# Moving router and norms to GpSimd, spreading the softmax's inverse by TensorE, and reordering ScalarE's and GpSimd's slots

## The chip, the cores and the metric

One core of a Trainium2 chip runs the whole kernel. The metric is the device time in microseconds; lower is better. An execution here takes about 6.4 milliseconds.

## The reference

The input x is 8 images of 56 x 56 positions with 64 channels, fp32. Four blocks follow each other, each added to its input:

1. Attention over regions. The normed input is projected to q, k and v. Each image has 7 x 7 regions of 64 positions. For each region the 4 best regions are chosen by the product of mean q and mean k. With 8 heads of 8 channels, each of the 64 queries scores the 256 keys of these four regions, keeps the **32 largest scores** (`jax.lax.top_k`), and takes the softmax over these 32 alone to mix the values. A 3 x 3 depthwise convolution of v is added, then an output projection.
2. A mixture of 8 experts over tokens: logits by a router, softmax, the two largest probabilities, scaled so that their sum is 1; out = t + sum over experts of weight * (gelu(t @ w1 + b1) @ w2 + b2), with t the layer norm of the tokens.
3. A 3 x 3 convolution with weights of +1 and -1 on the normed input.
4. Another mixture of 8 experts, with a hidden size of 128 and a router with a bias, where the two largest probabilities are used as they are.

## The kernel before, in words

The image rows are cut into 56 strips of 8 rows (448 positions, 4 tiles of 112), seven strips an image. A strip holds 7 regions, so there are 392 regions. Time is laid out in **slots**: one region is selected a slot. Two strips (14 slots) are a turn, and a hardware loop runs over turns.

Five kinds of work share the slots:
- stage a (strip): norm, q/k/v projection, stores to DRAM;
- stage t (strip): choice of the four regions;
- stage b (region): gather k, v and q (sp_gather), scores on TensorE (pe_scores), copy to b_s (act_scores), selection on VectorE (dve_select: four rounds of MAX8 and MATCH_REPLACE8 on four blocks of 256 keys, where a selected score becomes GONE), softmax sum (act_sum: negated maximum, four exponentials of the 32 kept values with an accumulated sum) and exponentials of all scores (act_exp), then on GpSimd the inverse of the sum (pool_inverse, L493, a power of -1), the mask (pool_mask, L502: is the score GONE, times the inverse, four instructions since the inverse is a column for each block of heads), the product (pool_prob, L510), then the turn of the probabilities by TensorE in two halves (pe_turn L524, copies act_turn L532) and the values (pe_values L545, copy act_values L552);
- stage c0 (strip, a few slots later): depthwise convolution and output projection (step 0 of pe_c, L611 to L616), turned back to tokens (TURN), added to x (L816), norm, router (GATE, step 3, step 4), experts in groups (UP + g, DOWN + g), sum, second norm, split into bf16 parts (step 8, LOW);
- stage c1 (strip): binary convolution (L619 to L623), the same norm, router and experts, store.

What is done in which slot is a table, PLACES: for each engine a number per step. The whole part, taken modulo 7, is the slot; the fraction is the place in it. In `("c0", 4): 85.7` for VectorE, 85 is slot 1 modulo 7. Experts have their own rows: c0's groups stand in slots 86 and 87 (2 and 3 modulo 7), c1's in slots 110, 111 and 112 (5, 6 and 0). Each engine works through its list in order, and waits on semaphores. The order inside one slot r:
- VectorE: dve_select(r), then its steps. It waits for the scores of r and for the product of r-2 (b_prob), since b_r and b_v8 have two buffers.
- ScalarE: act_sum(r), act_exp(r), steps below 0.2, first copy of the turned probabilities of r-1, act_scores(r + 2), second copy, steps to 0.6, act_values(r - 1), the rest of the steps.
- TensorE: steps below 0.2, pe_turn(r - 1, 0), pe_scores(r + 2), pe_turn(r - 1, 1), steps to 0.6, pe_values(r - 1), the rest.
- GpSimd: pool_inverse(r), pool_mask(r), steps from 0.2 to 0.5, pool_prob(r), the rest.

On VectorE stages c0 and c1 have step 1 (tok = x + projection, mean and variance), step 2 (normalise, L247 and L251), step 3 (largest logit and subtraction), step 4 (router: L834 to L861, some 18 operations of 32 or 4 columns), step 7 (sum and second statistics). ScalarE's step 3 is the router's exponential (L728). An exponential after a GELU, and a GELU after an exponential, needs an ACT_TABLE_LOAD; plain copies do not.

## Time and profile before

| | |
|---|---|
| runs shown | 6418.39, 6423.66, 6434.80 us; median 6423.66 |
| profiled execution | 6440.11 us, its span 6438.2 us |
| busy: PE, DVE, ACT, POOL | 4737.3, 5596.4, 4054.4, 4425.8 us |
| share of the span | 74%, 87%, 63%, 69% |
| granted TensorE clock | 0.73 of full over the span |
| chain that ended last | PE 29%, ACT 18%, issue 16%, DVE 15%, POOL 12% |
| HBM | 34 GB/s over the span |

The busy times are of one profiled execution; an engine's instructions may overlap each other, and such overlap is counted once in the busy share, but twice where the time of a group of instructions is summed. The chain is the one followed back from the last instruction; "issue" in it is time in which the profile shows no wait.

### The profile page before, as it was taken

How to read it: one execution, taken by the hardware profiler on the slowest of the kernel's cores; microseconds unless marked ns; L12 is line 12 of the kernel's file. 1: busy time of each engine (PE TensorE's matmuls, PEld its weight loads, DVE VectorE, ACT ScalarE, POOL GpSimd, SP SyncE). 2: the span in 40 equal slices, each digit the busy share in tenths (PEclk: the TensorE clock that was granted, in tenths of full speed). 3: DMA queues.
4: the chain of work that ended last, by engine and by line, in shares of the span. 5: the costliest groups of instructions: out<-in, count | busy, mean ns of one | idle time of the engine just before them, and what ended most of it. 6: DMA issues, size and time to landing. Idle time of an engine off the chain costs nothing.

```text
span 6438.2 us, 135940 instructions
## 1 busy us (share of the span) xinstructions
PE 4737.3 (74%) x26938; PEld 2880.6 (45%) x26938; DVE 5596.4 (87%) x24453; ACT 4054.4 (63%) x10222; POOL 4425.8 (69%) x3986
## 2 busy tenths in 40 slices
PE   3566777777777777777777777777777777777776
PEld 1333444444444444444444444444444444444444
DVE  1999999988989998999989898989999899999941
ACT  2455666666666666666666666666666666666643
POOL 1667776767677776767677677767776777777742
PEclk9666767777777777777777777777777777777777
DMA  4111111111111111111111111111111111111100
GB/s 75 39 31 42 34 40 34 40 32 42 30 41 34 39 35 34 40 32 43 32 42 30 40 36 36 38 33 40 32 43 31 43 31 32 30 30 34 33 11 10
DMA packets 585501, 229.09 MB, mean 36 GB/s; under 512 B 481152, under 2 KB 580224, under 8 KB 584576
## 3 DMA queue, kind: packets, MB, share of 16 engines
q1 hardware_dynamic: 584576, 219.25, 15.4%
q8 instruction: 276, 4.52, 0.3%
q14 instruction: 649, 5.32, 0.3%
HBM read 150.14 MB, written 68.80 MB: 34 GB/s over the span
## 4 chain that ended last, share of the span: by engine, by line
PE 29%; ACT 18%; issue 16%; DVE 15%; POOL 12%; ACTq 0%; DVEq 0%; POOLq 0%; DMA 0%; SPq 0%
DVE b_v L452 7%; POOL b_r L502 5%; PE y_ps L685 4%; DVE b_r L463 4%; PE h_ps L611 4%; POOL c_h L762 4%; ACT b_x L478 3%; PE a_ps L666 3%; PE pT_ps L524 3%; PE o_ps L545 2%; ACT b_e L485 2%; ACT L737 2%; PE h_ps L666 2%; POOL b_rec L493 2%; ACT L478 2%
## 5 line engine op out<-in xcount | busy, mean ns | idle before, releaser
L463 DVE MATCH_REPLACE8 b_r<-b_v,b_r 128x256 f32<-128x256 f32 x4704 | 1879.1, 416 | 0.0
L502 POOL TENSOR_SCALAR b_r<-b_r,b_rec 128x256 f32<-128x256 f32 x1568 | 1777.1, 1147 | 119.6 <-POOL b_rec L493 119.6
L452 DVE MAX8 b_v<-b_r 128x8 f32<-128x256 f32 x4704 | 1649.2, 418 | 0.0
L524 PE MATMUL pT_ps<-k_ident,b_e 128*128 128x128 f32 x3136 | 669.9, 352 | 776.3 <-ACT b_pT L532 688.3
L493 POOL TENSOR_TENSOR b_rec<-b_den,k_mone 128x4 f32<-128x4 f32 x392 | 400.5, 1022 | 1153.5 <-ACT b_x L478 1150.2
L762 POOL TENSOR_TENSOR c_h<-c_h,c_cb 128x448 f32<-128x448 f32 x672 | 760.9, 1133 | 503.9 <-ACT c_cb L739 503.0
L524 PEld LDWEIGHTS pT_ps<-k_ident,b_e 128*128 128x128 f32 x3136 | 472.6, 180 | 1161.2 <-issue 1136.2
L510 POOL TENSOR_TENSOR b_e<-b_e,b_r 128x1024 f32<-128x1024 f32 x392 | 923.5, 2356 | 18.0 <-POOL b_r L502 14.4
L685 PE MATMUL y_ps<-k_w,c_h 128*112 128x64 f32 x5376 | 776.1, 298 | 181.1 <-POOL c_h L762 177.9
L685 PEld LDWEIGHTS y_ps<-k_w,c_h 128*112 128x112 f32 x5376 | 706.5, 210 | 404.1 <-issue 403.0
L452 DVE MAX8 b_v<-b_s 128x8 f32<-128x256 f32 x1568 | 551.1, 415 | 318.0 <-POOL b_e L510 201.2
L532 ACT ACTIVATE b_pT<-pT_ps 128x512 f32<-128x512 f32 x784 | 469.9, 599 | 432.3 <-PE pT_ps L524 432.0
L485 ACT ACTIVATE b_e<-b_s,b_nm 128x256 f32<-128x256 f32 x1568 | 662.1, 493 | 0.0
L463 DVE MATCH_REPLACE8 b_r<-b_v,b_s 128x256 f32<-128x256 f32 x1568 | 624.7, 413 | 0.0
L666 PE MATMUL h_ps<-c_xT,k_w 128*128 128x448 f32 x672 | 525.4, 879 | 74.0 <-issue 67.5
L425 PE MATMUL s_ps<-b_k,b_q 32*128 32x256 f32 x3136 | 559.5, 484 | 24.2 <-DMA b_q<-q_d 24.2
L435 ACT ACTIVATE b_s<-s_ps 128x512 f32<-128x512 f32 x784 | 427.0, 603 | 117.5 <-PE s_ps L425 117.3
L478 ACT ACTIVATE b_x<-b_v,b_nm 128x32 f32<-128x32 f32 x1568 | 484.2, 310 | 9.5
L666 PE MATMUL a_ps<-c_xT,k_w 128*128 128x448 f32 x672 | 451.5, 765 | 0.0
L425 PEld LDWEIGHTS s_ps<-b_k,b_q 32*128 32x128 f32 x3136 | 336.3, 233 | 155.7 <-issue 119.6
L463 DVE MATCH_VALUE_LOAD b_r<-b_v,b_r 128x8 f32 x4704 | 405.3, 86 | 0.0
L737 ACT ACTIVATE c_h<-h_ps,k_b 128x448 f32<-128x448 f32 x336 | 212.8, 633 | 271.2 <-PE h_ps L666 268.5
(146 smaller groups left out, 7904.9 us busy)
## 6 DMA issues: line engine op xcount, KB each, us to landing
q_d<-a_qe SPq DMA_DIRECT2D x56, 448.0 KB, 4.2
b_k<-k_d SPq DMA_DIRECT2D x1568, 16.0 KB, 2.0
b_v<-v_d SPq DMA_DIRECT2D x1568, 16.0 KB, 2.0
b_q<-q_d SPq DMA_DIRECT2D x392, 64.0 KB, 2.1
c_win<-vpad_d SPq DMA_DIRECT2D x56, 145.0 KB, 2.8
c_hm<-cpad_d SPq DMA_DIRECT2D x56, 145.0 KB, 2.3
vpad_d<-a_vT SPq DMA_DIRECT2D x56, 116.0 KB, 3.7
c_win<-vpad_d SPq DMA_DIRECT2D x56, 116.0 KB, 2.7
```

The costliest lines, as they stand in the source:

```text
L425: last = pe.matmul(s_ps[g][:, t * NKEY:(t + 1) * NKEY], b_q[r % RING][part, 2 * t:2 * t + 2, :].rearrange("c h t -> c (h t)"), b_k[r % RIN ...
L452: top = dve.max(out=b_v8[p][:, t, 8 * rnd:8 * rnd + 8], in_=src[:, t, :])
L463: last = dve.match_replace(out=b_r[p][:, t, :], in_to_replace=b_v8[p][:, t, 8 * rnd:8 * rnd + 8], in_values=src[:, t, :], imm_value=GONE)
L478: last = act.activation(b_x8[:, t, :], b_v8[p][:, t, :], ACT.Exp, bias=b_nm[p][:, t:t + 1], accum_out=b_den[p][:, t:t + 1])
L485: last = act.activation(b_e[p][:, t, :], b_s[p][:, t, :], ACT.Exp, bias=b_nm[p][:, t:t + 1])
L493: pool.tensor_tensor(out=b_rec[p][:, :], in0=b_den[p][:, :], in1=k["mone"][:, 0:HP], op=ALU.pow).then_inc(b_inv, 1)
L502: last = pool.tensor_scalar(out=b_r[p][:, t, :], in0=b_r[p][:, t, :], scalar1=GONE, scalar2=b_rec[p][:, t:t + 1], op0=ALU.is_le, op1=ALU.mult)
L510: pool.tensor_tensor(out=b_e[p][:, :, :], in0=b_e[p][:, :, :], in1=b_r[p][:, :, :], op=ALU.mult).then_inc(b_prob, 1)
L524: last = pe.transpose(pT_ps[:, col:col + 128], b_e[p][:, t, c * 128:(c + 1) * 128], k["ident"][:, :])
L666: pe.matmul(bank[:, 0:STRIP], w1[layer][:, g, :], D["xT"][:, :], start=True, stop=True).then_inc(S["h"], 1)
L685: last = pe.matmul(y_ps[0:TILE, t * C:(t + 1) * C], D["h"][g % 2][:, t * TILE:(t + 1) * TILE], w2[layer][:, g, :], start=False, stop=(g == ...
L762: pool.tensor_tensor(out=D["h"][g % 2][:, :], in0=D["h"][g % 2][:, :], in1=D["cb"][g % 2][:, :], op=ALU.mult).then_inc(S["hc"], 1)
```

## The change

- Stage b: the inverse of the sum moves from GpSimd to VectorE (dve_inverse, a reciprocal), placed inside the selection of the **next** region, after its first four MAX8. The mask on GpSimd is one instruction over 1024 elements without the inverse. The product is therefore not normalised; instead TensorE spreads the inverses of a region over the rows of o_ps beside the values (four products with the identity), act_values copies 256 columns, and GpSimd multiplies a whole strip once (c0 step NORM).
- ScalarE and GpSimd: the steps and the turned probabilities of region r-1 come first, act_sum(r), act_exp(r) and act_scores(r + 2), or pool_mask(r) and pool_prob(r), last.
- Stages c0 and c1: addition (ADD), norm and residual are done on GpSimd. Router: ScalarE copies the logits into a padded tile, VectorE only takes the eight largest and replaces the two largest (MAX8 and MATCH_REPLACE8 over 14 columns); GpSimd subtracts, and after one exponential over both copies takes the difference, which leaves the two chosen; then sum, inverse and split into bf16 parts, nine small operations in a chain.
- PLACES: norm transposes and gates one slot earlier on TensorE and ScalarE, the layer-0 convolution from before the turned probabilities of slot 1 to behind its values, the router's exponential from 0.7 to 0.3 of a slot (of slot 6 to slot 5, and of slot 3 to slot 2), and others as in the diff.

```diff
-        b_rec = [sb(f"b_rec{i}", [128, HP]) for i in range(2)]
+        b_rec = [sb(f"b_rec{i}", [128, HP]) for i in range(RING)]
-        b_at = [sb(f"b_at{i}", [128, 2, RH, W]) for i in range(2)]
+        b_at = [sb(f"b_at{i}", [128, 4, RH, W]) for i in range(2)]
...
+        def dve_inverse(dve, tau, r):
+            reg = tau * SLOTS + r
+            dve.wait_ge(b_sum, reg + 1)
+            alone(dve)
+            dve.reciprocal(b_rec[r % RING][:, :], b_den[r % 2][:, :]).then_inc(b_inv, 1)
...
+                if rnd == 0 and older is not None:
+                    dve_inverse(dve, tau, older)
...
-            for t in range(HP):
-                last = pool.tensor_scalar(out=b_r[p][:, t, :], in0=b_r[p][:, t, :], scalar1=GONE, scalar2=b_rec[p][:, t:t + 1],
-                                          op0=ALU.is_le, op1=ALU.mult)
-            last.then_inc(b_msk, 1)
+            pool.tensor_scalar(out=b_r[p][:, :, :], in0=b_r[p][:, :, :], scalar1=GONE, scalar2=None,
+                               op0=ALU.is_le).then_inc(b_msk, 1)
...
             pe.wait_ge(b_att, reg + 1)
             alone(pe)
+            pe.wait_ge(b_inv, reg + 1)
+            alone(pe)
+            for t in range(HP):
+                pe.matmul(o_ps[32 * t:32 * t + VH, 128:256], b_rec[r % RING][:, t:t + 1].broadcast_to([128, VH]), k["ident"][:, :],
+                          start=True, stop=True)
...
-                           o_ps[:, 0:128].rearrange("c (j h q) -> c j h q", j=2, h=RH), ACT.Copy).then_inc(b_att, 1)
+                           o_ps[:, 0:256].rearrange("c (j h q) -> c j h q", j=4, h=RH), ACT.Copy).then_inc(b_att, 1)
...
-                    pe.wait_ge(b_att, NWIN * (s + 1) + 1)
+                    pe.wait_ge(b_nrm, s + 1)
...
-                act.activation(D["p"][:, :, :], D["l"][:, :, :], ACT.Exp).then_inc(S["ex"], 1)
+                act.activation(D["p"][:, :, :, :], D["l"][:, :, :, :], ACT.Exp).then_inc(S["ex"], 1)
...
+            if step == NORM:
+                pool.wait_ge(b_att, NWIN * (s + 1) + 1)
+                pool.tensor_tensor(out=b_at[i][:, 0:2], in0=b_at[i][:, 0:2], in1=b_at[i][:, 2:4], op=ALU.mult).then_inc(b_nrm, 1)
+            if step == ADD:
+                pool.wait_ge(S["x_in"][i], LOADS[layer] * (tau + 1))
+                pool.wait_ge(S["pr"], s + 1)
...
+                pool.tensor_tensor(out=D["tok"][i][:, :, :], in0=D["x"][i][:, :, :], in1=D["pr"][:, :, :], op=ALU.add).then_inc(S["free"], 1)
...
+                normalise(pool, D["tok"][i], D["mv"], D["rs"], D["xn"], S["sub"], s + 1, S["norm"])
...
+            if step == 3:
+                pool.wait_ge(S["top"], s + 1)
+                alone(pool)
+                pool.tensor_tensor(out=D["l"][:, :, :, :], in0=D["lr"][:, :, :, 0:NE],
+                                   in1=D["pv"][:, :, 6:7].unsqueeze(1).broadcast_to([TILE, 2, NT, NE]), op=ALU.subtract).then_inc(S["ls"], 1)
+            if step == 4:
...
+                pool.wait_ge(S["ex"], s + 1)
+                alone(pool)
+                pool.tensor_tensor(out=cw[:, :, :], in0=p[:, 0], in1=p[:, 1], op=ALU.subtract).then_inc(mix, 1)
...
             if step == 3:
                 dve.wait_ge(S["lc"], s + 1)
                 alone(dve)
...
+                lr, pv = D["lr"], D["pv"]
                 for t in range(NT):
-                    ins = dve.max(out=D["pv"][:, t, :], in_=p[:, t, :])
+                    ins = dve.max(out=pv[:, t, :], in_=lr[:, 0, t, :])
                 link(ins)
                 for t in range(NT):
...
+                    ins = dve.match_replace(out=lr[:, 1, t, :], in_to_replace=pv[:, t, :], in_values=lr[:, 0, t, :], imm_value=GONE)
+                ins.then_inc(S["top"], 1)
...
-                ("c1", 0): 101.66, ("c1", 9): 115.66},
-            dve={("a", 1): 4.9, ("a", 5): 10.9, ("t", 2): 61.8,
-                 ("c0", 1): 80.7, ("c0", 2): 81.7, ("c0", 3): 83.7, ("c0", 4): 85.7, ("c0", 7): 89.7,
-                 ("c1", 1): 104.66, ("c1", 2): 106.66, ("c1", 3): 108.66, ("c1", 4): 109.66, ("c1", 7): 114.66},
-            pool={("a", 1): 4.9, ("c0", 1): 80.7, ("c0", 2): 81.7, ("c0", 7): 89.7, ("c0", 8): 91.7, ("c1", 1): 104.66},
+                ("c1", 0): 101.66, ("c1", 9): 114.66},
+            dve={("a", 1): 4.9, ("a", 5): 10.9, ("t", 2): 60.8,
+                 ("c0", 1): 79.7, ("c0", 3): 81.7, ("c0", 7): 88.7,
+                 ("c1", 1): 103.7, ("c1", 3): 106.7, ("c1", 7): 113.7},
+            pool={("a", 1): 5.2, ("c0", NORM): 78.2, ("c0", ADD): 79.25, ("c0", 1): 80.2, ("c0", 3): 82.25, ("c0", 4): 82.35,
+                  ("c0", 7): 89.2, ("c0", 8): 90.2,
+                  ("c1", ADD): 103.25, ("c1", 1): 104.2, ("c1", 3): 107.25, ("c1", 4): 107.35},
             pe={("a", 3): 7.9, ("a", 4): 8.9, ("t", 1): 59.8,
-                ("c0", 0): 78.1, ("c0", TURN): 78.5, ("c0", TURNED): 78.68, ("c0", 2): 81.66, ("c0", GATE): 82.05,
...
+                ("c0", 0): 78.62, ("c0", TURN): 78.7, ("c0", TURNED): 78.8, ("c0", 2): 80.75, ("c0", GATE): 81.05,
+                ("c0", GATED): 81.31, ("c0", 4): 85.85, ("c0", 8): 92.3, ("c0", LOW): 92.55, ("c0", LOWED): 92.69,
+                ("c1", 0): 102.1, ("c1", TURN): 102.5, ("c1", TURNED): 102.68, ("c1", 2): 105.695, ("c1", GATE): 106.05,
...
-                 ("c0", 0): 78.3, ("c0", TURN): 78.52, ("c0", 2): 81.68, ("c0", GATE): 82.12, ("c0", 3): 83.7,
...
+                 ("c0", 0): 78.64, ("c0", TURN): 78.72, ("c0", 2): 80.77, ("c0", GATE): 81.12, ("c0", 3): 82.3,
+                 ("c0", 4): 85.87, ("c0", 8): 92.35, ("c0", LOW): 92.57,
+                 ("c1", 0): 102.3, ("c1", TURN): 102.52, ("c1", 2): 105.7, ("c1", GATE): 106.12, ("c1", 3): 107.3,
...
                     for r in range(SLOTS):
                         before = on and (r >= 1 or not first)
-                        if on:
-                            act_sum(act, b, r)
-                            act_exp(act, b, r)
                         steps(act, "act", n, lo, r, fs, 0, 0.2)
                         if before:
                             act_turn(act, b, r - 1, 0)
-                        if on and (r + 2 < SLOTS or not last):
-                            act_scores(act, b, r + 2)
-                        if before:
                             act_turn(act, b, r - 1, 1)
...
                         steps(act, "act", n, lo, r, fs, 0.6, 1)
+                        if on:
+                            act_sum(act, b, r)
+                            act_exp(act, b, r)
+                            if r + 2 < SLOTS or not last:
+                                act_scores(act, b, r + 2)
...
                     for r in range(SLOTS):
+                        steps(pool, "pool", n, lo, r, fs, 0, 1)
                         if on:
-                            pool_inverse(pool, b, r)
                             pool_mask(pool, b, r)
-                        steps(pool, "pool", n, lo, r, fs, 0.2, 0.3)
-                        steps(pool, "pool", n, lo, r, fs, 0.3, 0.5)
-                        if on:
                             pool_prob(pool, b, r)
-                        steps(pool, "pool", n, lo, r, fs, 0.5, 1)
```

## Rows read from the trace of the kernel before

**Rows 1.** Stretch 3000 to 4000 us: length, busy by engine (count), clock, DMA, GB/s.

```profile
3000.00:4000.00 1000.00, 757.00 (x4368) 462.21 (x4367) 901.51 (x3924) 658.71 (x1652) 713.77 (x642) 0.72 0.16 36
```

**Rows 2.** Power L493, once a region: whole span, then two stretches (length, busy, count).

```profile
L493 POOL TENSOR_TENSOR b_rec<-b_den,k_mone x392: 1006/1016/1274, 170.9 to 6164.2; 128x4 f32<-128x4 f32 x196
...
3000.00:4000.00 1000.00, 64.24 (x63) 0.72 0.16 36
5200.00:5400.00 200.00, 14.28 (x14) 0.77 0.15 35
```

**Rows 3.** VectorE in order of time, one selection and the steps behind it.

```profile
3063.07 1.41 DVE L452 MAX8 b_v<-b_s 128x8 f32<-128x256 f32 x4 [0.53 <-issue]
...
3074.60 2.23 DVE L247 TENSOR_TENSOR c_xn<-c_tok,c_mv 112x256 f32<-112x256 f32 x1
...
3082.46 1.41 DVE L452 MAX8 b_v<-b_s 128x8 f32<-128x256 f32 x4
...
3091.10 1.41 DVE L452 MAX8 b_v<-b_r 128x8 f32<-128x256 f32 x4
```

**Rows 4.** VectorE's waits, 3000 to 4000 us: total us, times, longest.

```profile
DVE b_v L452 <- POOL b_e L510: 46.9, 9, 5.7
```

**Rows 5.** ScalarE in order of time, sums and first or second copies.

```profile
3063.07 0.19 ACT L475 ACTIVATE b_nm<-b_v 128x4 f32<-128x4 f32 x1
...
3070.47 0.60 ACT L532 ACTIVATE b_pT<-pT_ps 128x512 f32<-128x512 f32 x1
...
3080.07 0.21 ACT L475 ACTIVATE b_nm<-b_v 128x4 f32<-128x4 f32 x1
...
3089.67 0.60 ACT L532 ACTIVATE b_pT<-pT_ps 128x512 f32<-128x512 f32 x1 [5.14 <-PE pT_ps L524]
...
3101.00 0.20 ACT L475 ACTIVATE b_nm<-b_v 128x4 f32<-128x4 f32 x1
```

**Rows 6.** ScalarE's waits, 3000 to 4000 us, then (last row) 5200 to 5900 us.

```profile
ACT b_pT L532 <- PE pT_ps L524: 69.0, 49, 5.2
...
ACT b_nm L475 <- DVE b_v L452: 46.3, 9, 5.7
ACT c_h L737 <- PE h_ps L666: 42.7, 22, 3.5
...
ACT b_nm L475 <- DVE b_v L452: 45.7, 18, 4.8
```

**Rows 7.** ScalarE by line and shape, 3000 to 4000 us: busy, mean ns, idle before.

```profile
L485 ACT ACTIVATE b_e<-b_s,b_nm 128x256 f32<-128x256 f32 x252 | 106.4, 493 | 0.0
L478 ACT ACTIVATE b_x<-b_v,b_nm 128x32 f32<-128x32 f32 x252 | 77.8, 310 | 1.5
...
L737 ACT ACT_TABLE_LOAD x45 | 57.7, 1283 | 0.8
```

**Rows 8.** TensorE in order of time: turns and scores at either clock.

```profile
3020.88 0.66 PE L524 MATMUL pT_ps<-k_ident,b_e 128*128 128x128 f32 x4
3021.47 1.13 PE L425 MATMUL s_ps<-b_k,b_q 32*128 32x256 f32 x8
...
3031.92 1.06 PE L524 MATMUL pT_ps<-k_ident,b_e 128*128 128x128 f32 x4
3032.91 2.08 PE L425 MATMUL s_ps<-b_k,b_q 32*128 32x256 f32 x8
```

**Rows 9.** GpSimd by line and shape, 3000 to 4000 us.

```profile
L502 POOL TENSOR_SCALAR b_r<-b_r,b_rec 128x256 f32<-128x256 f32 x252 | 285.8, 1148 | 19.2 <-POOL b_rec L493 19.2
L510 POOL TENSOR_TENSOR b_e<-b_e,b_r 128x1024 f32<-128x1024 f32 x64 | 150.7, 2355 | 2.9 <-POOL b_r L502 2.9
...
L775 POOL CAST c_x<-c_xm 112x256 bf16<-112x256 f32 x9 | 3.6, 396 | 1.8 <-POOL c_xm L251 1.8
```

**Rows 10.** GpSimd in order of time: first and last operation of step 8.

```profile
3076.51 0.80 POOL L247 TENSOR_TENSOR c_xm<-c_x,c_mv 112x256 f32<-112x256 f32 x1
...
3080.14 0.72 POOL L782 TENSOR_TENSOR c_x<-c_xd,c_x 112x256 bf16<-112x256 f32 x1
```

132 lines of the change are left out of this document (55 added, 77 removed).

## The prediction

> **What bounds the kernel now.** I read the stretch view first [rows 1], because the page's shares are means: between 3000 and 4000 us every stage is on, VectorE is busy 90% of the time, GpSimd 71%, ScalarE 66%, TensorE 76% at a granted clock of 0.72, a mix of its two levels, 1.2 and 2.4 GHz. VectorE looks like the bound. The count of regions gives the pace [rows 2]: 63 in 1000 us, 15.87 us a region slot, 111.1 us a strip of seven. In the last part, where stage a has ended, 14 slots take 200 us, 100 us a strip. Of 392 slots the full load holds from about slot 112 to 394 (40.3 strips) and the lighter one to 462 (9.7 strips).
>
> A selection runs from 3063.07 to 3074.60 [rows 3]: 11.5 us, 81 us a strip. So VectorE would have 30 us a strip to spare, and the change takes most of that off it. The question is what holds it back at present. Its waits name GpSimd's product of probabilities [rows 4]: 46.9 us in nine strips, one wait of 5.2 us a strip. Behind that stands ScalarE. The selection that began at 3082.46 had its last maxima at about 3092.5 [rows 3], and ScalarE began that region's softmax only at 3101.00 [rows 5]: 8.5 us late. ScalarE waits for VectorE 46.3 us in nine strips [rows 6], once a strip; the rest of its idle time is spent on TensorE (turned probabilities 69.0, hidden layer 42.7). So **ScalarE's own chain is 111.1 - 5.1 = 106.0 us a strip**, only 5 us under the pace, though it is busy for 73. VectorE hides its lateness only because a region's result is wanted a whole slot later (two buffers). In the last part the same sum is 100 - 6.5 = 93.5 us [rows 2, 6].
>
> **VectorE.** Removed: both norms, the additions of tokens and the router's arithmetic. One such block lies between 3074.60 and 3082.46, 7.9 us, 2.2 of it a subtraction that stood against GpSimd's product [rows 3]. With the other layer I take 13.5 us a strip. Added: a reciprocal a region (0.2 each, the nearest being the router's small ones) and four small replacements a layer, 2.6 us together. Its pace would be 7 x 11.7 + 9 = 91 us a strip. But the edit also moves a wait: the reciprocal of region r-1 stands after the first four maxima of region r (1.4 us), and waits for ScalarE's sum r-1. VectorE may now be ahead of ScalarE by some 3 us, not by a slot. And ScalarE's sum r wants VectorE's last maxima, 8.6 us after that reciprocal. Behind the waiting reciprocal the whole rest of the selection is queued.
>
> **ScalarE's chain, the term that decides.** It stays in order: older work of slot r, then sum r, exponentials r, scores r+2. What each edit adds to its 106.0 us a strip:
> 1. *Table loads, +5.1.* The router's exponential now stands at 0.3 of slots 5 and 2, between GELUs at 0.15 and 0.35; before, it stood last and shared the load of the region's softmax. That makes two more loads for each of two layers, 4 x 1.283 [rows 7]. Nothing hides them: ScalarE is the chain.
> 2. *Turning region r at once, +7.5 in the five slots with GELUs.* Before, from the end of a sum (3063.07 + 1.5 without a load) to the end of the second copy (3071.07) went 6.5 us [rows 5], since the product had been ready for long. Now: exponentials 1.69 [rows 7], product 2.36 [rows 9], 0.2 of signals, a turn of 0.6, scores 1.1, a turn 0.6, a copy 0.6, makes 7.2 at the full clock; with 1.0, 2.1 and 1.0 for the TensorE pieces at the low one 9.0 [rows 8]. So +0.7 to +2.5 a slot; I take 1.5, the clock now being mixed. Bounds 3.5 to 12.5. The GELU at 0.15 with its load fills the wait for the product, else it would be more.
> 3. *The two slots without GELU at the head, +2.4*, by the same sum without the filler, less what they waited before; bounds 0 and 5.
> 4. *The layer-0 convolution behind the values, +1.5.* Before, ScalarE did a sum and exponentials (3080.07 on) under it and then waited 5.14 us [rows 5]. Now it stands idle for all of it, 5.2 to 8.0 us; bounds 0 and 2.9.
> 5. *Two copies at 0.35 and 0.57 of slot 1 that wait for each other through TensorE, +0.9*; bounds 0 and 1.5.
> 6. *Wider values copy (256 columns for 128), +0.7.* The four spreading products on TensorE (0.3 to 0.5 us a region) start before the second copy is there; I cost them at nothing, their cover being that copy.
> 7. *GpSimd in slot 6, +4.0.* At 0.2 stand the splitting of layer 0 (3076.51 to 3080.86, 4.35 us [rows 10]) and the norm of layer 1 (one power of 1.02, two passes of some 0.7, small ones and signals, 2.9), ahead of the first hidden product. That comes 8 us after the region's product, TensorE's first down-projection of the slot some 4 us later than ScalarE would let it, and the third GELU stands behind it. Bounds 2 and 5.
> 8. *A credit, -2.4.* The hidden products no longer stand behind mask and product of the same region; of the 42.7 us in which ScalarE waited for h_ps (4.7 a strip [rows 6]) I take half. Bounds 0 and -4.7.
>
> The sum is +19.7, bounds +6.6 and +32.7 with all at one end.
>
> **GpSimd.** The four masks of 1148 ns and the power of 1.02 us a region become one mask of 1024 elements. No row shows this form. Below: four casts of 256 elements, 1.6 us; above: the four masks, 4.6 [rows 9]. I take 1.6, since what has no operand from a column in memory is nearest to the cast. It lies under ScalarE's late softmax at either value in four slots, and is late by up to 1.8 us in slots 3, 6 and 0. The router (nine small operations, some 3.9 us with their waits, twice), the additions, norms and the product NORM come to 13 us; the engine is busy 79.3 - 39.2 + 11.2 + 13 = 64 us a strip. Its cover is ScalarE's chain of 125. The router's wait for the exponential holds up the second hidden product of slots 5 and 2; what is late there is the end of TensorE's slot, 16 us in, and the next GELU has 2 us in hand.
>
> **SyncE.** The DMAs are the same; one store stands a slot earlier, beside a DMA share of 0.16 [rows 1]. Nothing.
>
> **The numbers.** ScalarE's chain becomes 106.0 + 19.7 = 125.7 us a strip, above VectorE's 91: 14.6 more than 111.1. In the last part 93.5 + 19.7 = 113.2, 13.2 more. 40.3 x 14.6 + 9.7 x 13.2 = 588 + 128 = 716 us. The profiled execution took 6440.1 us (span 6438.2); the median of the runs shown is 0.26% below it. 7156 x 0.9974 = 7138, and with a few us back in the tail, where VectorE's router chain was in the path, **7130 us**. With each term at its lower end the strip takes 112.6 us: about 6500 us. At the upper end 138.7 us: 7800 us.
>
> Of table loads the Trainium skill (ScalarE: Activation LUTs, What ACT_TABLE_LOAD costs) says that a switch costs a drain besides, 2.66 us in all. By that the four would cost 10.6 us a strip, and the time would be 7400 us. The rows speak against it here: 252 activations behind such loads had 1.5 us of idle time before them in all [rows 7].
>
> **Rivals.** *VectorE sets the pace (17%), the faster side.* If ScalarE keeps within 3 us of VectorE in the five light slots (2 to 6), only slots 0 and 1 stay long (18.8 and 21.5 us at the full clock) and the others take 5 x 11.7 + 8: 107 us a strip, and 100 in the last part. That is 40.3 x -4.1 = -165: 6260 us. It decides at 13 us for ScalarE's light slots, where I find 15 to 20. For it speaks the 30 us that VectorE gains, against it row upon row of ScalarE waiting for TensorE, with just one wait a strip for VectorE.
> *The waits change places (6%).* TensorE stays at 2.4 GHz since its gaps become shorter, the credit is whole, and 6440 us stays. The granted 0.72 speaks against it: the wait for the product is a new gap of 2 to 3 us in each slot.
> *GpSimd's single mask costs as much as four (10%).* Then it is late in three slots, 1.8 us each: 5.4 x 50 = 270, so 7400 us. If the mask does not become shorter the change does not do what it says.
> The forecast has 67%. About 0.3%, 20 us, is what a measurement of this kernel can tell from no change.
>
> Faster by more: 17% and 1% of the places case, 0.18. Within 0.3%: 0.05. Slower: 0.77. The forecast's own range is 6650 to 7500. To leave out no more than two in ten the lower end goes down to 6350, which takes in the waits case and the lower bounds, but not the whole of the faster rival: 6350 to 7500.
>
> **What would show it.** Right: in the changed profile ScalarE has 14 table loads a strip (before, 45 of nine strips stand at the GELUs, and as many bring the exponential back: 10), its first softmax operation hardly waits for VectorE's maxima, VectorE idles at its new reciprocal for ScalarE's sum (some 30 us a strip, the longest in slot 2, behind the convolution), VectorE's share falls to 75%, and 63 slots take over 1100 us. The mask reads 1.2 to 1.8 us. Wrong: VectorE stays above 95% busy and ScalarE waits for its maxima in most slots; then the chain of step 2 was shorter than the rows made it, or lay beside something. If the time is right but ScalarE waits for GpSimd's products, step 7 was too small and step 2 too large.

## The result, and the profile after

The changed kernel takes **7863.5 us** in the median of four runs (7858.9 to 7873.7), the kernel before, run beside it, 6426.6 us (6418.4 to 6434.8): ratio 1.2238, interval 1.2217 to 1.2259, 1437 us more. The direction was forecast. The time was not: 7130 us stood in the forecast, and 7500 as its upper end.

The page of the changed kernel: its span, the busy times of part 1, TensorE's clock from part 2 and five groups of part 5 (busy, mean ns of one, idle before, what ended it):

```profile
span 7860.9 us, 141661 instructions
...
PE 5294.8 (67%) x30074; PEld 3185.7 (41%) x30074; DVE 5008.0 (64%) x22719; ACT 4439.8 (56%) x10426; POOL 4023.5 (51%) x4042
...
PEclk9565666666666666666666666666666666677666
...
L522 PE MATMUL pT_ps<-k_ident,b_e 128*128 128x128 f32 x3136 | 846.2, 424 | 1371.3 <-POOL b_e L508 1354.4
L508 POOL TENSOR_TENSOR b_e<-b_e,b_r 128x1024 f32<-128x1024 f32 x392 | 922.3, 2353 | 1631.9 <-ACT b_e L494 1617.3
...
L443 DVE RECIPROCAL b_rec<-b_den 128x4 f32<-128x4 f32 x392 | 68.6, 175 | 2356.4 <-ACT b_x L487 2356.3
L501 POOL TENSOR_SCALAR b_r<-b_r 128x1024 f32<-128x1024 f32 x392 | 1087.0, 2773 | 741.2 <-DVE b_r L472 736.8
...
L530 ACT ACTIVATE b_pT<-pT_ps 128x512 f32<-128x512 f32 x784 | 468.7, 598 | 1457.0 <-PE pT_ps L522 1457.0
```

No engine is the bound any more: the fullest, TensorE, is busy 67% of the span at a low clock, VectorE fell from 87% to 64%. The four large idle sums are links of one ring. ScalarE's copy waits for TensorE's turn, the turn for GpSimd's product, the product for ScalarE's exponentials, and VectorE's reciprocal for ScalarE's sum. All of a region's softmax is now done in one line, at each slot anew.

The same stretch of 1000 us as in [rows 1], and the masks in it, which count regions as the powers of [rows 2] did:

```profile
3000.00:4000.00 1000.00, 693.70 (x3961) 417.89 (x3960) 652.35 (x2952) 589.50 (x1370) 532.08 (x536) 0.67 0.13 29
...
3000.00:4000.00 1000.00, 144.21 (x52) 0.67 0.13 29
```

There were 63 regions, now there are 52: 19.2 us a slot for 15.9. Over all 392 regions, from the first mask at 174.6 us to the last at 7564.4, a slot takes 18.90 us; before, from 170.9 to 6164.2, it took 15.33. Those 3.57 us times 391 are 1396 of the 1437.

Waits of the changed kernel, 3000 to 4000 us (total, times, longest):

```profile
DVE b_rec L443 <- ACT b_x L487: 327.7, 44, 14.4
...
POOL b_e L508 <- ACT b_e L494: 219.4, 36, 15.6
ACT b_pT L530 <- PE pT_ps L522: 182.0, 97, 2.8
PE pT_ps L522 <- POOL b_e L508: 153.8, 51, 5.9
```

ScalarE's wait for turned probabilities was 69.0 us, 49 times, in [rows 6]. It now comes at nearly every copy. The 46.3 us in which it waited for VectorE's maxima are no longer in the list. The engines in order of time (start, length; in brackets the idle time before):

```profile
3004.00 0.20 ACT L484 ACTIVATE b_nm<-b_v 128x4 f32<-128x4 f32 x1
...
3006.74 1.69 ACT L494 ACTIVATE b_e<-b_s,b_nm 128x256 f32<-128x256 f32 x4
...
3009.12 2.35 POOL L508 TENSOR_TENSOR b_e<-b_e,b_r 128x1024 f32<-128x1024 f32 x1 [0.16 <-POOL b_r L501]
...
3011.86 1.08 PE L522 MATMUL pT_ps<-k_ident,b_e 128*128 128x128 f32 x4 [2.46 <-POOL b_e L508]
...
3012.99 0.60 ACT L530 ACTIVATE b_pT<-pT_ps 128x512 f32<-128x512 f32 x1 [1.06 <-PE pT_ps L522]
3016.04 0.60 ACT L530 ACTIVATE b_pT<-pT_ps 128x512 f32<-128x512 f32 x1 [2.46 <-PE pT_ps L522]
...
3069.10 0.63 ACT L716 ACTIVATE c_yT<-h_ps,out_bias 64x448 f32<-64x448 f32 x1 [6.77 <-PE h_ps L620]
...
3077.50 0.18 DVE L443 RECIPROCAL b_rec<-b_den 128x4 f32<-128x4 f32 x1 [14.06 <-ACT b_x L487]
```

From the end of the sum (3006.84) to the end of the second copy (3016.64) go 9.8 us; six such stretches in a row read 9.2 to 10.1, where I had 7.2 at the full clock and 9.0 at the low one. The mean over the 1000 us is 9.4; before, it was 6.8. In five of the six the two copies start 3.05 or 3.06 us apart, as here, and the first turn takes 1.08 us: TensorE turns both halves at the low level. At the convolution ScalarE stands 6.77 us, and VectorE stands 14.06 at the reciprocal.

**Two halves of a slot.** For what follows I cut ScalarE's slots between 3000 and 3992 us into two: A from the start of the negated maximum to the end of the second turned copy, B from there to the next negated maximum. Means in us, worked out from each run's timeline (the changed kernel's A and B sum to 19.5 where the count of masks gives 19.2, so 0.3 us is what such a mean is good for):

| kernel | us | A | B |
|---|---|---|---|
| before (62 slots) | 6432 | 8.97 | 6.93 |
| changed (50) | 7864 | 11.91 | 7.61 |
| before with new orders (45) | 8785 | 15.81 | 6.00 |
| changed, old orders (52) | 7423 | 8.74 | 9.76 |
| changed, old places (53) | 7435 | 12.27 | 5.89 |
| changed, idle transposes (52) | 7595 | 11.03 | 7.73 |
| combination (63) | 6259 | 8.84 | 6.56 |

"Orders" are those of ScalarE and GpSimd. "Old places" are those of router, norms and first convolution; step 7, step 8 and the store keep the places of the change.

### The profile page after: what moved, and what is told of

It is laid out like the page before. It is cut to its first block and busy times, and to the rows that moved or that the text cites. A ratio compares the mean times of both kernels' runs of the same rounds, so it can differ in the third digit from the quotient of the medians.

```text
span 7860.9 us, 141661 instructions
## 1 busy us (share of the span) xinstructions
PE 5294.8 (67%) x30074; PEld 3185.7 (41%) x30074; DVE 5008.0 (64%) x22719; ACT 4439.8 (56%) x10426; POOL 4023.5 (51%) x4042
## 5 line engine op out<-in xcount | busy, mean ns | idle before, releaser
L522 PE MATMUL pT_ps<-k_ident,b_e 128*128 128x128 f32 x3136 | 846.2, 424 | 1371.3 <-POOL b_e L508 1354.4
L443 DVE RECIPROCAL b_rec<-b_den 128x4 f32<-128x4 f32 x392 | 68.6, 175 | 2356.4 <-ACT b_x L487 2356.3
L501 POOL TENSOR_SCALAR b_r<-b_r 128x1024 f32<-128x1024 f32 x392 | 1087.0, 2773 | 741.2 <-DVE b_r L472 736.8
L522 PEld LDWEIGHTS pT_ps<-k_ident,b_e 128*128 128x128 f32 x3136 | 549.0, 213 | 1919.9 <-issue 1919.9
L689 PE MATMUL y_ps<-k_w,c_h 128*112 128x64 f32 x5376 | 812.3, 308 | 412.1 <-POOL c_h L813 404.7
L689 PEld LDWEIGHTS y_ps<-k_w,c_h 128*112 128x112 f32 x5376 | 760.2, 221 | 623.9 <-issue 617.6
L425 PE MATMUL s_ps<-b_k,b_q 32*128 32x256 f32 x3136 | 803.2, 661 | 24.2 <-DMA b_q<-q_d 24.2
L670 PE MATMUL a_ps<-c_xT,k_w 128*128 128x448 f32 x672 | 563.3, 941 | 0.0
L425 PEld LDWEIGHTS s_ps<-b_k,b_q 32*128 32x128 f32 x3136 | 455.8, 314 | 216.9 <-issue 150.1
L741 ACT ACTIVATE c_h<-a_ps,k_b 128x448 f32<-128x448 f32 x336 | 213.2, 635 | 371.6 <-PE a_ps L670 369.7
```

Of the source, the lines that this page charges most:

```text
L425: last = pe.matmul(s_ps[g][:, t * NKEY:(t + 1) * NKEY], b_q[r % RING][part, 2 * t:2 * t + 2, :].rearrange("c h t -> c (h t)"), b_k[r % RIN ...
L501: pool.tensor_scalar(out=b_r[p][:, :, :], in0=b_r[p][:, :, :], scalar1=GONE, scalar2=None, op0=ALU.is_le).then_inc(b_msk, 1)
L522: last = pe.transpose(pT_ps[:, col:col + 128], b_e[p][:, t, c * 128:(c + 1) * 128], k["ident"][:, :])
L670: pe.matmul(bank[:, 0:STRIP], w1[layer][:, g, :], D["xT"][:, :], start=True, stop=True).then_inc(S["h"], 1)
L689: last = pe.matmul(y_ps[0:TILE, t * C:(t + 1) * C], D["h"][g % 2][:, t * TILE:(t + 1) * TILE], w2[layer][:, g, :], start=False, stop=(g == ...
L741: act.activation(D["h"][g % 2][:, :], (h_ps, a_ps)[g % 2][:, 0:STRIP], ACT.Gelu, bias=b1[layer][:, g:g + 1]).then_inc(S["ge"], 1)
```

## The experiments

Except for e15, each kernel was run once beside the kernel before (6427.5 to 6432.4 us). Where PLACES is edited, the diffs here show only the entries that differ.

**e1, ScalarE's old order in the changed kernel.**

```diff
+                        if on:
+                            act_sum(act, b, r)
+                            act_exp(act, b, r)
                         steps(act, "act", n, lo, r, fs, 0, 0.2)
                         if before:
                             act_turn(act, b, r - 1, 0)
+                        if on and (r + 2 < SLOTS or not last):
+                            act_scores(act, b, r + 2)
+                        if before:
                             act_turn(act, b, r - 1, 1)
...
-                        if on:
-                            act_sum(act, b, r)
-                            act_exp(act, b, r)
-                            if r + 2 < SLOTS or not last:
-                                act_scores(act, b, r + 2)
```

> The changed kernel with ScalarE's old order alone: sum and exponentials of region r first, then the slot's steps, with the scores' copy between the two copies of the turned probabilities of r-1. GpSimd keeps the new order. Theory A (ScalarE's chain is the pace, and the new order puts softmax, product and turn of one region behind each other in it): the wait for the product and the gap between the two copies leave the chain, some 2.5 to 3.5 us a slot, so about 6700 to 7000 us, and ScalarE's waits for turned probabilities fall from 25 us a strip below 12. Rival B (VectorE's slack is gone, since the reciprocal stands inside the selection): the reciprocal still waits there, 7700 us or more.

Measured: 7334.4 us, 529 less, though not down to the 6700 to 7000 of theory A. The wait for turned copies fell from 182.0 to 34.2 us, the clock rose from 0.673 to 0.705. But 906 us stayed, in new waits: VectorE's router maxima for ScalarE's logits (84.6 us), GpSimd's addition of tokens for ScalarE's copy (92.9). So the order costs, and is not all.

**e3, the reciprocal behind the third round of maxima** (`rnd == 0` becomes `rnd == 2`).

> The changed kernel with the reciprocal of region r-1 behind the maxima of the third round of region r instead of the first, so that VectorE can be 5.8 us further ahead before it waits. Theory A: VectorE's wait shrinks, but ScalarE is the chain and the time stays within 1% of 7860 us. Rival B: VectorE's wait is the cost, and the time falls by 30 us a strip, to 6400 to 6800 us.

Measured: 7852.5 us, 11 less, under the bound of 0.3%. But VectorE's wait hardly shrank (312.5 us for 327.7 between 3000 and 4000 us), where theory A had it shrinking: VectorE stands until the sum comes, behind the first round or behind the third. So the place of the reciprocal is not the cause. What the standing itself costs, this run doesn't show.

**e4, the router's exponentials at the end of their slots.**

```diff
-("c0", 3): 82.3,
+("c0", 3): 82.7,
-("c1", 3): 107.3,
+("c1", 3): 107.7,
-("c0", 4): 82.35,
+("c0", 4): 83.58,
-("c1", 4): 107.35}
+("c1", 4): 108.58}
```

> The changed kernel with the router's exponential at 0.7 of its slot, behind the slot's GELUs, and GpSimd's nine small operations a slot later behind its hidden products. Theory A: 10 table loads a strip for 14, 5.1 us and two exponentials' waits less, so 250 to 400 us less than 7860. Rival B: the loads lie beside VectorE's wait, no more than 1% less.

Measured: 7883.2 us, no gain. The loads fell as meant, from 103 to 74 in 1000 us. ScalarE of that run, in a slot that had held a load, an exponential and a load:

```profile
3089.82 0.60 ACT L530 ACTIVATE b_pT<-pT_ps 128x512 f32<-128x512 f32 x1 [2.46 <-PE pT_ps L522]
3091.31 0.64 ACT L741 ACTIVATE c_h<-a_ps,k_b 128x448 f32<-128x448 f32 x1 [0.90 <-PE a_ps L670]
...
3094.38 0.38 ACT L555 ACTIVATE b_at<-o_ps 128x256 f32<-128x256 f32 x1 [2.00 <-PE o_ps L548]
```

The second copy ends at 3090.42 and the values copy starts at 3094.38, 3.96 us; in the changed kernel the same distance is 4.02 (3086.56 to 3090.58). Two loads of 1.28 us went and waits for TensorE of 0.90 and 2.00 came. These loads lay beside TensorE's work. (GpSimd's router moved too in this run, and TensorE's wait for the product grew from 153.8 to 215.9 us, so it doesn't price the loads alone.)

**e5, eight idle transposes ahead of each wait for the product.**

```diff
-            if half == 0:
-                pe.wait_ge(b_prob, reg + 3)
-                alone(pe)
             pe.wait_ge(b_ptc, 2 * reg + half + 1)
             alone(pe)
+            if half == 0:
+                for j in range(8):
+                    pe.transpose(pT_ps[:, (j % 4) * 128:(j % 4) * 128 + 128], k["ident"][:, :], k["ident"][:, :])
+                pe.wait_ge(b_prob, reg + 3)
+                alone(pe)
```

> The changed kernel with eight idle transposes of the identity on TensorE before it waits for the region's product (they write a bank that is written again afterwards, so the result is the same). If the wait for the product is what brings the granted clock down, and the turns and scores behind it take 2.46 us between the copies for that reason alone, the clock rises from 0.67 and the time falls by 1 to 2 us a slot, 400 to 700 us less than 7860. If the clock does not follow from that gap, or the copies set the pace, 7860 us or up to 1 us a slot more.

Measured: 7595.3 us, 268 less, where 400 to 700 were expected; granted clock 0.752 for 0.673. TensorE's turns in that run, 3000 to 4000 us, behind them the idle ones:

```profile
L524 PE MATMUL pT_ps<-k_ident,b_e 128*128 128x128 f32 x432 | 94.0, 357 | 97.1 <-POOL b_e L508 92.1 <-ACT b_pT L532 4.9
L518 PE MATMUL pT_ps<-k_ident 128*128 128x128 f32 x432 | 83.7, 359 | 0.0
```

The mean of one transpose of a turn is 357 ns for 424, and half A 11.03 us for 11.91. Useless work on TensorE makes the kernel faster here, so part of the cost is the clock. The eight undo it only in part: in 18 of the 52 slots the copies still start 3.05 us apart. In 24 they start less than 1.95 us apart, and there the time from sum to second copy is 8.3 us in the mean, for 9.4 in the changed kernel and 6.8 before. So where the clock is back, more than half of the growth is still there.

**e2, both old orders; e6, the first convolution back at its places too; e7, the reciprocal late as well.** The edit of e2 beside e1's, then that of e6 (TensorE's entries, ScalarE's, GpSimd's):

```diff
-                        steps(pool, "pool", n, lo, r, fs, 0, 1)
                         if on:
                             pool_mask(pool, b, r)
+                        steps(pool, "pool", n, lo, r, fs, 0, 0.5)
+                        if on:
                             pool_prob(pool, b, r)
+                        steps(pool, "pool", n, lo, r, fs, 0.5, 1)
...
-("c0", 0): 78.62, ("c0", TURN): 78.7, ("c0", TURNED): 78.8,
+("c0", 0): 78.1, ("c0", TURN): 78.5, ("c0", TURNED): 78.68,
-("c0", 0): 78.64, ("c0", TURN): 78.72,
+("c0", 0): 78.3, ("c0", TURN): 78.52,
-("c0", NORM): 78.2,
+("c0", NORM): 77.9,
```

> Both engines in the order of the kernel before, all else of the change kept: ScalarE as in e1_act_order (7334 us), GpSimd mask first, steps below 0.5, product, rest. Theory A (one chain of ScalarE, TensorE and GpSimd is the pace, and any of them behind its turn lengthens it): the product no longer stands behind all steps of its slot, and VectorE's waits for it (7 us, once or twice a strip) go: 6800 to 7100 us. Rival C (after ScalarE's order the rest is the longer slots themselves, whatever GpSimd does first): 7250 to 7400 us.

> As e2_act_pool_order, and the layer-0 convolution with its turn back in the places of the kernel before (78.1, 78.5, 78.68 on TensorE, 78.3 and 78.52 on ScalarE, GpSimd's product over the strip at 77.9). Theory A: ScalarE does a sum and exponentials under the convolution again, for which it now waits 7.2 us a strip: 3 to 6 us a strip less, 150 to 300 us less than e2. Rival C: as long, or within 1% of e2, because TensorE has the same work and turns come later in its place.

> As e6_conv_early, and the reciprocal behind the maxima of the third round. With ScalarE in the old order a sum can be up to 8 us late without a wait of VectorE if the reciprocal comes late enough. Theory A: in this order VectorE's slack counts again, 0 to 150 us less than e6. Rival C: within 0.5% of e6, as e3 was of the changed kernel.

Measured: 7422.8, 7267.4 and 7253.6 us. GpSimd's old order gave nothing on top of ScalarE's: e2 is 88 us slower than e1, above even the rival's 7400. The convolution's place gave 155 us, the low end of the 150 to 300 expected, the reciprocal 14. With half A back at 8.74 in e2, about as before, B had grown to 9.76. The waits of e7 say where:

```profile
DVE c_pv L867 <- ACT c_lr L729: 151.6, 16, 15.7
...
DVE c_st L849 <- POOL c_tok L766: 96.6, 16, 8.4
```

VectorE stands up to 15.7 us in front of router and statistics steps whose input is not there, each at a place one or two slots too early for the old order, and its next selection is queued behind.

**e8, stage b's part alone in the kernel before** (reciprocal on VectorE behind the third round, one mask of 1024, spread by TensorE, wide copy, product NORM at 77.9; orders, router and places untouched).

```diff
-            for t in range(HP):
-                last = pool.tensor_scalar(out=b_r[p][:, t, :], in0=b_r[p][:, t, :], scalar1=GONE, scalar2=b_rec[p][:, t:t + 1],
-                                          op0=ALU.is_le, op1=ALU.mult)
-            last.then_inc(b_msk, 1)
+            pool.tensor_scalar(out=b_r[p][:, :, :], in0=b_r[p][:, :, :], scalar1=GONE, scalar2=None,
+                               op0=ALU.is_le).then_inc(b_msk, 1)
```

> The kernel before with the stage b part of the change alone: reciprocal on VectorE (behind the third round's maxima), one mask of 1024 elements, the inverse spread by TensorE, 256 columns copied, one product a strip at 77.9. Router, norms, orders and places are those before. Theory A: GpSimd's mask is 2.8 us for 4.6 and the power of 1.0 and its wait are gone from ahead of the product, so the one stall of 5 us a strip shrinks: 6200 to 6400 us. Rival C: VectorE's added reciprocals and TensorE's added products eat it, 6400 to 6500 us.

Measured: 6694.4 us, 267 more than before and outside both theories, with GpSimd's busy time down from 714 to 542 in 1000 us and VectorE's up from 902 to 961. VectorE and GpSimd of that run in order of time:

```profile
3044.01 3.55 DVE L860 TENSOR_TENSOR c_z<-c_pv 112x4 f32<-112x4 f32 x1
3044.47 2.07 POOL L759 TENSOR_TENSOR b_at<-b_at 128x896 f32<-128x896 f32 x1
3046.51 2.76 POOL L502 TENSOR_SCALAR b_r<-b_r 128x1024 f32<-128x1024 f32 x1
...
3048.01 0.19 DVE L863 TENSOR_TENSOR c_cw<-c_cw,c_rz 112x32 f32<-112x32 f32 x1
3048.24 1.07 DVE L866 CAST c_cw<-c_cw 112x32 bf16<-112x32 f32 x1
...
3049.44 2.34 POOL L509 TENSOR_TENSOR b_e<-b_e,b_r 128x1024 f32<-128x1024 f32 x1 [0.16 <-POOL b_r L502]
3049.57 2.24 DVE L868 CAST c_cw<-c_cwd 112x32 bf16<-112x32 f32 x1
```

The cast of 3048.24 ends at 3049.31, the mask at 3049.27; the cast of 3049.57 ends at 3051.81, the product at 3051.78. So it is with all 21 of these casts that took over 0.6 us between 3000 and 4000 us: each ends within 0.1 us of a GpSimd instruction. The addition at the top doesn't: it lasts 3.55 us and ends at 3047.56, 1.0 us into the mask, as do all seven long ones of its line. Before, these casts took 225 and 270 ns in the mean, now 676 and 1633. The Trainium skill (SBUF — State Buffer, Who interferes with whom) says that VectorE and GpSimd share one pair of ports under an exclusive lock. The rows agree for the casts. The multiplication of 3048.01 lies wholly inside the mask and took 0.19 us, in nine strips of nine, so not every operation is caught; and a plain wait for the end of GpSimd's instruction doesn't explain the addition.

**e9, the same with the mask in four immediates of 256; e10, with four in the old form** (a column of -1 as second operand, so the attention part comes out with its sign turned).

> The kernel before with the stage-b part (6694 us), and in it the mask of a region in four instructions of 128x256 instead of one of 128x1024, the same immediate. In the run before this, VectorE's small router operations stretched beside GpSimd's one long mask (2.76 us): c_cw CAST 1633 ns instead of 270, c_z 2800 instead of 479, some 88 us more in 1000 us. Theory A, the length of the single instruction makes the stretch (VectorE gets its turn between two GpSimd instructions): here no stretch is over 0.8 us a piece, the small operations come back under 500 ns in the mean, 6400 to 6500 us. Theory B, the form with an immediate alone keeps VectorE out however it is cut: the means stay at 700 to 2800 ns and the time at 6650 to 6750 us; each piece would take about 0.7 us.

> The same kernel with the mask in the form of before: four instructions of 128x256 with a second operand that is a column of the table (a column of -1, so the attention part comes out with its sign turned), 1148 ns each before. Theory A (length of one instruction): as with four immediates, but GpSimd pays 4.6 us instead of 2.8: 6400 to 6500 us. Theory B (the immediate form keeps VectorE out): this form lets it in, VectorE's small operations are back at 200 to 500 ns, 6400 to 6500 us, while the run with four immediates stays at 6650 or more. If neither brings the time back (both at 6650 and over), the stretch is not what the stage-b part costs, and its longer GpSimd and TensorE work is.

Measured: 6585.4 and 6481.1 us. VectorE's lines other than the selection and the reciprocal sum up (3000 to 4000 us, per seven regions) to 20.5 us before, 29.7 in e8, 26.7 in e9, 23.5 in e10. The time follows in that order: 6432, 6694, 6585, 6481. Neither theory had it whole: cutting the instruction helps by 109 us, the form by 104 more. e9 was expected at 6400 to 6500 by the one and over 6650 by the other, e10 at 6400 to 6500 by both. The old form costs GpSimd 4 x 1.153 us a region and is still the better neighbour of a busy VectorE; why, these runs don't tell.

**e11, e7 with router and norms also at the places of before**, on GpSimd still (and stage t's step 2 and GpSimd's step 1 of stage a with them; step 7, step 8 and the store stay where the change put them).

```diff
-("c0", 1): 79.7, ("c0", 3): 81.7,
+("c0", 1): 80.7, ("c0", 3): 83.7,
-("c1", 1): 103.7, ("c1", 3): 106.7,
+("c1", 1): 104.66, ("c1", 3): 108.66,
-("c0", 1): 80.2, ("c0", 3): 82.25, ("c0", 4): 82.35,
+("c0", 1): 80.7, ("c0", 3): 83.7, ("c0", 4): 84.75,
-("c1", 1): 104.2, ("c1", 3): 107.25, ("c1", 4): 107.35}
+("c1", 1): 104.7, ("c1", 3): 108.66, ("c1", 4): 109.25}
...
```

(TensorE and ScalarE: steps 2, GATE, GATED and 4 as in the kernel before, ScalarE's step 3 at 84.3 and 109.1.)

> The changed kernel with both old orders, the old places of the first convolution and the inverse behind the third round (7254 us), and now the router and the norms (still on GpSimd) at the places of before, a slot and more later, so that each step's input is there before its engine comes to it. Theory A, the early places cost what VectorE waits at its router and statistics steps (152 + 97 us of 1000, and 100 for ScalarE's negated maximum behind them): these waits go, 6350 to 6700 us. Theory B, GpSimd's queue is what binds (the mask waits for VectorE in order, and the router work stands in between): 7000 to 7250 us, with GpSimd's steps now waited for elsewhere.

Measured: 6264.6 us, 989 less than e7, below the range of theory A and **below the kernel before**. Of the two waits of e7 the list has nothing left; half B fell from 8.53 to 6.56.

**e12, e11 without stage b's part**: router and norms on GpSimd alone.

> As the run with the places of before, and stage b's inverse, mask and copy as in the kernel before too: what is left of the change is the router and the norms on GpSimd alone. VectorE had 901 us busy in 1000 before, about 106 us of them router, norm and combine that GpSimd now takes. Theory A, moving them is sound in itself and only the orders, places and the mask's form spoil it: 6050 to 6400 us. Theory B, GpSimd (714 us busy in 1000 before, most of it mask and products that the next region waits for) can't take them without delaying mask and product: 6600 to 7100 us. Against the run before in this call it also prices the stage-b part a second time.

Measured: 6874.2 us. GpSimd is busy 734 us of 1000 for 57 regions, 12.9 us a region; before 11.3, in e11 10.0. TensorE waits 102.8 us for its products (c_h), ScalarE 78.4 us for the hidden layer behind them. So the two moves need each other: stage b's part alone costs 267, the router's alone 444, both together gain 165. The likely reason, put together from e8 to e12 and not tried by itself: the first takes work off GpSimd and makes it a bad neighbour, the second takes away what suffers from that and fills the room.

**e13, the two new orders alone in the kernel before; e14, the changed kernel with only the places put back** (the entries of e6 and e11). GpSimd's part of e13:

```diff
+                        steps(pool, "pool", n, lo, r, fs, 0.2, 1)
                         if on:
                             pool_inverse(pool, b, r)
                             pool_mask(pool, b, r)
-                        steps(pool, "pool", n, lo, r, fs, 0.2, 0.3)
-                        steps(pool, "pool", n, lo, r, fs, 0.3, 0.5)
-                        if on:
                             pool_prob(pool, b, r)
-                        steps(pool, "pool", n, lo, r, fs, 0.5, 1)
```

> The kernel before with the two new orders alone: ScalarE does a slot's older work first and sum, exp and scores' copy last, GpSimd does the steps first and inverse, mask and product last. Theory A, the orders are what costs, since each region then goes ScalarE's exp, GpSimd's product, TensorE's turn, ScalarE's copy in one line with nothing beside it: ScalarE waits for the turned probabilities more than 20 us a strip, the granted clock falls under 0.70, 7200 to 7900 us. Theory B, the orders cost only together with the new places and the router on GpSimd: 6500 to 6900 us.

> The changed kernel with its new orders and only the places put back (router, norms and first convolution where the kernel before has them). Against the run with old orders and these places (6265 us) it prices the orders, against the changed kernel (7864 us) the places. Theory A, orders cost: 7300 to 7800 us, with VectorE's wait at the reciprocal and ScalarE's wait for the turned probabilities as in the changed kernel. Theory B, places cost: 6400 to 6900 us. If both must be wrong together (each alone costs little), this run is near 6600 and the one with the orders alone near 6600 too.

Measured: 8784.7 and 7435.4 us. One region of e13 in order of time:

```profile
3051.60 1.69 ACT L485 ACTIVATE b_e<-b_s,b_nm 128x256 f32<-128x256 f32 x4
3051.87 1.01 POOL L493 TENSOR_TENSOR b_rec<-b_den,k_mone 128x4 f32<-128x4 f32 x1 [7.05 <-ACT b_x L478]
...
3053.19 4.52 POOL L502 TENSOR_SCALAR b_r<-b_r,b_rec 128x256 f32<-128x256 f32 x4 [0.30 <-POOL b_rec L493]
...
3057.87 2.34 POOL L510 TENSOR_TENSOR b_e<-b_e,b_r 128x1024 f32<-128x1024 f32 x1 [0.16 <-POOL b_r L502]
...
3060.60 1.08 PE L524 MATMUL pT_ps<-k_ident,b_e 128*128 128x128 f32 x4 [6.52 <-POOL b_e L510]
3061.72 0.60 ACT L532 ACTIVATE b_pT<-pT_ps 128x512 f32<-128x512 f32 x1 [4.85 <-PE pT_ps L524]
3064.77 0.60 ACT L532 ACTIVATE b_pT<-pT_ps 128x512 f32<-128x512 f32 x1 [2.46 <-PE pT_ps L524]
```

From sum (3051.69) to second copy (3065.37) are 13.7 us, the power and the masks now in the line. This is the mechanism in full; the time lies 885 us above the upper end that I had given it. In e14 VectorE still waits 291.5 us at the reciprocal and ScalarE 221.8 us for turned copies, so those waits belong to the orders, and half A stays at 12.27.

**e15, the combination timed; e16, the combination with e5's idle transposes.**

> The combination again (stage b's part and router and norms on GpSimd from the change, orders and places from before, inverse behind the third round), timed: one look gave 6264.6 against 6430.1, a ratio of 0.974. Expected 6250 to 6280 us and a ratio of 0.972 to 0.977 if that look was an ordinary one.

> The combination with eight idle transposes of the table on TensorE ahead of each wait for the product, which gave 268 us in the changed kernel. Theory A, in the combination TensorE works right up to the turn (granted clock 0.78) and the eight only take its time, 0.07 us each at least: 6270 to 6400 us. Theory B, the clock at the turns still costs: 6100 to 6230 us, with a granted clock of 0.85 or more.

Measured: e15 6259.3 us in the median of five runs (6242.7 to 6275.9) against 6432.4, **ratio 0.9728, interval 0.9710 to 0.9747**; e16 6337.9 us, 79 more, at a granted clock of 0.811 for 0.782. Where the product is ready long before its turn, the eight only take time. Stretch and waits of e15, 3000 to 4000 us:

```profile
3000.00:4000.00 1000.00, 734.85 (x5013) 463.10 (x5012) 824.81 (x3746) 703.11 (x1717) 655.75 (x655) 0.79 0.16 37
```

```profile
POOL c_h L813 <- ACT c_cb L743: 251.9, 61, 9.9
...
PE pT_ps L522 <- ACT b_pT L530: 78.1, 35, 4.3
...
ACT b_pT L530 <- PE pT_ps L522: 48.1, 16, 4.9
DVE b_v L459 <- POOL b_e L508: 43.3, 11, 5.4
```

VectorE now has the spare time that the change was to give it (825 us busy for 902), and the regions come at 65 in 1000 us.

## Why the prediction was wrong in its size

**The account.** Four kernels have the moved work (times in us). The combination, at the top left, has neither new orders nor new places. It alone of the four has the reciprocal late, worth 11 and 14 us where that was tried (e3, e7):

| | old places | new places |
|---|---|---|
| old orders | 6259 | 7423 |
| new orders | 7435 | 7864 |

The moved work gains 173 us; new places cost 1164 with the old orders and 428 with the new; new orders cost 1176 at the old places and 441 at the new. Either spoils the kernel by about 1170 us, and the second then finds part of its price already paid. There is no single share of the 1437 us for each. In the kernel before, where the power and the four masks stand in the line too, the new orders alone cost 2352 us (e13). The halves of a slot keep orders and places apart: A goes up with the new orders (8.84 to 12.27, 8.74 to 11.91) wherever the places are, B with the new places (6.56 to 9.76, 5.89 to 7.61).

**The step that failed: step 2, turning a region at once in the five slots with GELUs.** I put +7.5 us a strip for it, 12.5 at most, and +2.4 for step 3, the two slots without. Half A grew from 8.97 to 11.91 us, 2.94 a slot, 20.6 a strip. By slot, counted from that of the convolution (means in us, 3000 to 4000; 9 strips before, 7 to 8 changed; slots 0 and 3 are those without a GELU at the head):

| | 0 | 1 | 2 | 3 | 4 | 5 | 6 |
|---|---|---|---|---|---|---|---|
| sum to second copy, before | 9.3 | 6.4 | 6.3 | 6.0 | 6.4 | 6.3 | 7.1 |
| sum to second copy, changed | 9.2 | 9.2 | 10.2 | 9.1 | 9.2 | 9.5 | 9.5 |
| half B, before | 8.6 | 2.7 | 5.2 | 9.0 | 7.1 | 6.6 | 8.9 |
| half B, changed | 16.2 | 4.4 | 5.3 | 3.4 | 5.8 | 8.3 | 9.8 |

The five slots of step 2 grew by 15.0 us, twice the term and above its upper bound. The two of step 3 grew by 3.0, near the 2.4. The rest of A's growth is table loads ahead of the sums (28 for 63 sums before, 37 for 52 now: 2.4 us a strip), which belong to step 1. What was mis-sized in step 2:
- *The clock.* I took the middle between the full and the low level, "the clock now being mixed". But TensorE's wait for the product stands right ahead of every turn (51 waits for 52 regions), and the turn mostly ran at the low level: copies 3.05 us apart in 42 of 50 slots. A plain slot took 9.2 us, 0.2 above my own sum at the low level. The average clock of the stretch (0.67) was no measure for the place. e5 gives 268 us for undoing part of this.
- *The filler.* I held that the GELU at 0.15 with its load fills the wait for the product, "else it would be more". The five slots with it grew by 3.0 us each, slot 3 without it by 3.1.
- *The mask.* At 2.77 us (2762 to 2784 ns) it lies nearer the upper bound of 4.6 than the 1.6 I took. My reason, that a mask without a column operand is nearest to the cast, was wrong. In 15 of the 51 regions the product starts right behind its mask, 0.56 to 1.26 us after the exponentials' end, as at 3009.12 (exponentials to 3008.43); in the others 0.07 to 0.09. Together that is 12.6 us in 1000, 1.7 a strip, and the most that the mask can have added to this line.

**Half B: the sum looks right and isn't.** Steps 1 and 4 to 8 come to +9.8, less the 5.1 us of waiting for VectorE that I took as going: +4.7 a strip. B grew from 6.93 to 7.61, +4.8. But 2.4 us of step 1 fell in half A, which leaves +2.3 for B, and the parts were off both ways.
- *The wait for VectorE* went, as forecast (slot 3 of the table: 9.0 to 3.4).
- *Steps 4 and 5*, the convolution and its copies, had +2.4, at most 4.4; B of the convolution's slot grew by 7.6. I had set the 5.14 us of the old wait off against the new idle time (46.7 us in seven strips, 6.7 each). But that slot's time from sum to second copy stayed at 9.2, since the region's own line now takes it up; under ScalarE's old order (e1) it fell to 4.0. The convolution's place gave 155 us in e6, 3 a strip, with the old orders.
- *Step 1* was wrong in its reason: the loads come to 103 for 52 regions, 13.9 a strip as forecast, but four fewer a strip bring no gain in e4. Against a dearer load I had read 252 activations "behind such loads"; only 28 of them stood behind one. The reading holds all the same: in the changed kernel a load starts at 3086.57, takes 1.28 us, and its exponential starts at 3087.87.
- *Step 7* had +4.0 in slot 6, which is 5 in the table, and B grew by 1.7 there; it wasn't tried alone.
- *Step 8*: of ScalarE's waits for the first hidden bank (h_ps) 0.9 us a strip is left of 4.7, but those for the other (a_ps) grew from 3.9 to 6.6.

**Together** a strip grew by 25.0 us (3.57 a slot) where I had 14.6: 7.5 of the difference is step 2, some 5 the convolution's slot, and the other terms give about 2 back. Such means are good to 0.3 us a slot, 2 a strip.

**The late part.** I gave it 113.2 us a strip. 27 regions in 500 us (6300 to 6800) are 129.6 and 28 in the 500 from 7000 on 125: it grew by 25 to 30 us, not 13.

**The rivals.** VectorE doesn't set the pace in the changed kernel. The 6260 us of that rival is what the combination takes, but by chance: there too VectorE is busy only 825 us of 1000. The room on VectorE was real, and the orders and places hid it. The rival in which the waits change places and the clock stays up was wrong: the clock fell from 0.72 to 0.67. The mask's length was between mine and the rival's, and its cost under the rival's 5.4 us a strip.

**What would show it.** Loads of 14 a strip: yes. ScalarE hardly waits for maxima: yes. The mask at 1.2 to 1.8 us: no, 2.77. VectorE waits at the reciprocal, longest behind the convolution: yes, though 44 us a strip (327.7 in 52 regions) rather than 30; by e3 the reciprocal's place is not the cause, and by e1, where the wait is 22.2 us in all, ScalarE's order is. VectorE's share 75%: it was 64%. 63 slots over 1100 us: about 1210.

## What to carry to other kernels

Work that waits for another engine's answer is cheap as long as a whole slot of other work lies between question and answer; an order that brings both into one slot put every engine's latency on the path here, and TensorE's low clock with it. When a change moves work and also re-times it, try the moved work at the old places first: here it was worth 2.7%, and the re-timing cost 1604 us on top and hid it. Such a line is priced at the level of the clock that the trace shows right behind the wait, and not at the mean clock. Two moves can each be a loss and together a gain, so a part that loses alone is not yet refuted.

## What the runs showed of the hardware

- GpSimd's comparison with an immediate on 128x1024 took 2773 ns, 2.7 ns a column; with a column as second operand, 128x256, 1148 ns, 4.5 a column; four immediates of 256 took 852 ns each in e9, 3.3 a column.
- Some of VectorE's small operations stretch beside GpSimd's long instructions (e8). A 112x32 cast took 2.24 us and ended with GpSimd's instruction, as all 21 long casts did (mean before 270 ns). A 112x4 addition took 3.55 us and ended 1.0 us into one (479 ns before). A 112x32 multiplication wholly inside one took 0.19 us.
- Eight idle transposes of about 0.36 us each raised the granted clock from 0.673 to 0.752 and shortened the kernel by 268 us where TensorE had stood right ahead of the turn (e5), and lengthened it by 79 us where it mostly had not (e16).
- A table load can go and the time stay: with 29 loads less in 1000 us (e4) the total was 20 us higher.
